# Order of turns of all five engines in a fused cross-attention kernel: one string per engine in place of planned times

## What is computed

```python
# layer 0 (H=16 heads of 16; _fq rounds to 8 bits)
h1 = _ln(x, ln1_g, ln1_b)
x = _attn(h1, h1, a1_wq, a1_wk, a1_wv, a1_wo, a1_bo, ...) + x      # self-attention, 1024 keys
h2 = _ln(x, ln2_g, ln2_b)
x = _attn(h2, context, a2_wq, a2_wk, a2_wv, a2_wo, a2_bo, ...) + x # 77 keys
a, g = jnp.split(_ln(x, ln3_g, ln3_b) @ ff_w1 + ff_b1, 2, axis=-1)
x = a * gelu(g) @ ff_w2 + ff_b2 + x
# layer 1 (16 query heads of 64, 4 key heads, rotary)
q, k = rope(rms(x) @ Wq), rope(rms(ctx) @ Wk)
x = x + softmax(q @ k.T / 8 + mask) @ v @ Wo
y = rms(x)
x = x + silu(y @ Wgate) * (y @ Wup) @ Wdown
```

## Time and profile before

| | us |
|---|---|
| median of 3 runs | 2564.54 (2559.13 to 2568.57) |
| profiled execution | 2568.71 |
| its span, first to last instruction | 2566.9 |
| PE busy in it | 2000.9 (78%) |
| DVE busy | 1802.5 (70%) |
| ACT busy | 1135.9 (44%) |
| POOL busy | 936.3 (36%) |
| mean granted clock of TensorE | 0.874 of full speed |

### The profile page before, as it was taken

How to read it: one execution, slowest core, us unless ns; L and a number is a source line. 1 busy time by engine, 2 the same in 40 slices (tenths; PEclk the granted TensorE clock), 3 DMA queues, 4 the chain that set the end, 5 groups by cost and what they waited for, 6 DMA issues and landing times.

```text
span 2566.9 us, 35318 instructions
## 1 busy us (share of the span) xinstructions
PE 2000.9 (78%) x10552; PEld 1439.1 (56%) x10552; DVE 1802.5 (70%) x3327; ACT 1135.9 (44%) x1906; POOL 936.3 (36%) x1629
## 2 busy tenths in 40 slices
...
GB/s 231 102 162 134 82 121 68 131 62 105 93 81 122 70 134 62 118 76 100 98 71 132 69 135 61 118 78 88 105 77 120 74 120 66 128 55 106 1 36 4
DMA packets 761645, 243.62 MB, mean 95 GB/s; under 512 B 675643, under 2 KB 757295, under 8 KB 761199
## 3 DMA queue, kind: packets, MB, share of 16 engines
q1 hardware_dynamic: 758127, 241.34, 46.3%
...
...
## 4 chain that ended last, share of the span: by engine, by line
PE 47%; DVE 21%; issue 9%; ACT 8%; SPq 5%; DMA 4%; POOL 4%; DVEq 0%; POOLq 0%; ACTq 0%
PE work L1394 21%; PE work L1404 16%; ACT E L899 4%; DVE scaled_row L1055 4%; DVE Pn L1062 3%; PE rowps L1465 3%; DMA PT<-Pn 3%; PE outps L1450 3%; POOL scs L797 2%; SPq L542 1%; DVE st L1078 1%; DVE hids L1202 1%; DVE scs L1144 1%; ACT hTs L875 1%; DVE scs L1216 1%
## 5 line engine op out<-in xcount | busy, mean ns | idle before, releaser
L1055 DVE TENSOR_SCALAR_CACHE_REDUCE scaled_row<-rowps,der 128x1024 uint8<-128x1024 f32 x512 | 654.0, 1277 | 386.8 <-PE rowps L1465 386.5
L899 ACT ACTIVATE E<-rowps,ebias,der 128x1024 f32<-128x1024 f32 x512 | 614.6, 1202 | 392.5 <-DVE scaled_row L1055 312.1
L731 POOL TENSOR_TENSOR rowden<-rowsum,raw 128x1 f32<-128x1 f32 x512 | 113.3, 221 | 943.6 <-ACT E L899 942.3
L1062 DVE TENSOR_SCALAR Pn<-E,rowinv 128x1024 int16<-128x1024 f32 x512 | 389.8, 761 | 89.0 <-DMA PT<-Pn 65.9
L1465 PE MATMUL rowps<-KC,QP 16*128 16x512 bf16 x1024 | 220.8, 428 | 209.5 <-ACT E L899 197.7
L734 POOL TENSOR_TENSOR rowinv<-rowden,minus 128x1 f32<-128x1 f32 x512 | 333.6, 651 | 92.4 <-POOL rowden L731 92.4
L1394 PE MATMUL work<-hTs,ff_w_sb 128*128 128x256 f32 x1024 | 259.9, 409 | 14.2 <-ACT hTs L875 14.2
L1465 PEld LDWEIGHTS rowps<-KC,QP 16*128 16x128 bf16 x1024 | 49.2, 92 | 375.5 <-ACT E L899 244.4
L1394 PEld LDWEIGHTS work<-hTs,ff_w_sb 128*128 128x128 f32 x1024 | 202.3, 204 | 60.0 <-issue 28.4
L1559 PE MATMUL work<-K,hids 128*128 128x154 f32 x1024 | 153.2, 301 | 31.6 <-DVE scs L1216 19.4
L1559 PEld LDWEIGHTS work<-K,hids 128*128 128x128 f32 x1024 | 136.9, 190 | 50.1 <-DVE scs L1216 26.3
...
## 6 DMA issues: line engine op xcount, KB each, us to landing
...
KC<-k_dram SPq DMA_DIRECT2D x128, 64.0 KB, 2.4
...
PT<-Pn SPq DMA_TRANSPOSE x512, 3.1
...
```

Source lines behind the costliest of these rows:

```text
L731: nc.gpsimd.tensor_tensor(rowden[:, n:n + 1], rowsum[:, n:n + 1], raw[:, DW1:DW1 + 1], ALU.mult).then_inc(row_den.sem, 1)
L899: nc.scalar.activation(E[:, slot, :], rowps[n % 2][:], ACT.Exp, bias=ebias[:, n:n + 1], scale=der[:, AL1:AL1 + 1], accum_out=rowsum[:, n:n ...
L1055: nc.vector.tensor_scalar(scaled_row[:, n % 2, :], rowps[n % 2][:], der[:, NAL1:NAL1 + 1], 3.0e38, ALU.mult, ALU.min, accum_out=ebias[:, n ...
L1062: nc.vector.tensor_scalar(Pn[:, n % 2, :], E[:, ring(n)[0], :], rowinv[:, n:n + 1], 255.0, ALU.mult, ALU.min).then_inc(row_round.sem, 1)
```

## The change

The planner goes: `places`, `AT`, `STARTS`, `BEHIND`, `PAIR_GAP` and `Beside` are removed, and an item keeps its name, its evicting engine and the number of its turns on PE. In their place stand five strings. Each letter gives one turn to one part of that engine: p, l, h are pre, low and high; r and v rows and values on PE; b and n maxima and roundings on DVE, s the sums of high's softmax, now a part of its own with its own semaphore; e and o exponentials and outputs on ACT; i inverses on POOL; t the row turns of SP. `take_turns` runs them. Every `yield` with a time becomes a bare `yield`. The banks follow the order of the starts in PE's string. Pre before step 0, and step 0 with its setup, are still merged by times (`by_time`), with pre's times kept in `PRE_AT`. A part that a step lacks is skipped in the string.

```diff
+PRE_ITEMS = [("tr", "A", 1), ("q", "A", 1), ("k", "A", 1), ("v", "A", 2)]
...
-BEHIND = {("high", "down"): ("low", "g", 0.1)}
-STARTS = {"pre": 2.0, "low": 2.0 * LAG + 3.5, "high": 0.5}
-US_PER_HALF = 1.85
-PAIR_GAP = 2.0
...
+TURNS = {
+    "PE": (
+        "vrhhhrrphprprvpphrrhhhhllhrhhrhhhhrhvlrrvlhhhrllhhrhhhhrhllrhrhhhrvrlrlvhrllhhhhvrrlllllhlrllhrhhlrv"
+        "rlllllrrhrrllrl"),
+    "DVE": (
+        "nnpbpnbbnhnbbhnbbhnnhhhlbhhbhhhnhbnlhnhssnbnbhssllbnbhhnblnlbbnnbhbbnnlhllnlbllnblblnnhblnnlhbhhbbnn"
+        "nblbnnhbbnllbl"),
+    "ACT": ("eeepeeppeehpoeeeeehhhllhehheoleheheeeeoehllhleehhhllelleeelleellleoee"),
+    "POOL": ("iipiihpiiliiilhhhiliihhhlhhiiippiiiihiillilliiilhhhlhiiiiiii"),
+    "SP": ("tttthlhlhhtlttpthhthtttptttttttttppttttttttttth"),
+}
...
+PRE_AT = {"tr": (4.0, 4.9), "q": (5.5, 6.9), "k": (6.3, 7.8), "v": (7.2, 8.7)}
...
-AT, ORDER = places(2 * ROWT - 1.5)
+def item_order():
+
+    begins = {c: {sum(x[2] for x in ITEMS[c][:i]): i for i in range(len(ITEMS[c]))} for c in ITEMS}
+    turn, out = {c: 0 for c in ITEMS}, []
+    for letter in TURNS["PE"]:
+        c = PARTS_OF.get(letter)
+        if c:
+            if turn[c] in begins[c]:
+                out.append((c, begins[c][turn[c]]))
+            turn[c] += 1
+    return out
...
+def take_turns(order, parts):
+
+    for part in parts.values():
+        next(part)
+    for letter in order:
+        if letter in parts:
+            next(parts[letter], None)
+    assert all(next(part, "end") == "end" for part in parts.values())
...
+        def run_step(parts, eng, v, order, attention, setup, pre, low, high, sums=None):
...
+            use = dict(attention) if parts["attn"] or parts["old"] else {}
+            for letter, part, d in (("p", pre, LEAD), ("l", low, -1), ("h", high, -2), ("s", sums, -2)):
+                if parts[PARTS_OF[letter]] and part:
+                    use[letter] = part(eng, v + d, runs)
+            take_turns(order, use)
...
             for n in range(4):
-                yield at("sc2", 2 * n + 1) + 1
+                yield
                 l_diff.wait(act, u, n + 1)
...
-            yield from beside_each_other(sums(0), scores(1))
-            yield from beside_each_other(sums(1), products())
+            yield from scores(1)
+            yield from products()
...
+        def high_sums(dve, u, runs):
+
+            for n in range(4):
+                yield
+                h_exp.wait(dve, u, n + 1)
+                nc.vector.tensor_reduce(lsum[:, 1, n, :], sc1[:, n], AX.X, ALU.add).then_inc(h_sums.sem, 1)
+                h_sums.wait(dve, u, n + 1)
+                nc.vector.reciprocal(rsum[:, 1, n, :], lsum[:, 1, n, :]).then_inc(recip_ready.sem, 1)
```

More of the change, by code:

```diff
@@ L60 @@
+    + [("pt1", "A", 1), ("pt1", "D", 1), ("pt1", "A", 1), ("pv1", "D", 4), ("tr3", "A", 1)]
+    + [("gate", "A", 1)] * 4 + [("up", "D", 1)] * 4 + [("down", "D", 1)])
 ITEMS = {"pre": PRE_ITEMS, "low": LOW_ITEMS, "high": HIGH_ITEMS}
-STARTS = {"pre": 2.0, "low": 2.0 * LAG + 3.5, "high": 0.5}
 BANKS = 3
-US_PER_HALF = 1.85
-PAIR_GAP = 2.0
+PARTS_OF = {"p": "pre", "l": "low", "h": "high", "s": "high"}
+TURNS = {
[9 more added lines that the diff above has]
+}
@@ L462, in all_steps @@
             loop(U + 1, U + 2, high=True)
-        def side(parts, eng, v, pre=None, low=None, high=None, setup=None):
+        def run_step(parts, eng, v, order, attention, setup, pre, low, high, sums=None):
             runs = [c for c in ITEMS if parts[c]]
             if parts["setup"]:
-                return Beside(setup(), later(pre(eng, v + LEAD, runs)))
-            return Beside(*[f(eng, v + d, runs) for c, d, f in (("pre", LEAD, pre), ("low", -1, low), ("high", -2, high))
-                            if parts[c] and f])
+                by_time(*attention.values(), setup(), later(pre(eng, v + LEAD, runs)))
+                return
+            use = dict(attention) if parts["attn"] or parts["old"] else {}
[3 more added lines that the diff above has]
+            take_turns(order, use)
         def ring(n):
@@ L688, in step @@
             def step(v, parts):
[L689 to L692 removed]
+                run_step(parts, sp, v, TURNS["SP"], {"t": attn_sync(sp, v, parts)}, setup_sync, pre_sync, low_sync, high_sync)
                 if parts["setup"]:
@@ L847, in step @@
             def step(v, parts):
-                beside = side(parts, pool, v, pre_pool, low_pool, high_pool, setup_pool_part)
-                if parts["attn"] or parts["old"]:
-                    attn_pool(pool, v, parts, beside)
-                beside.rest()
+                run_step(parts, pool, v, TURNS["POOL"], {"i": inverses(pool, v, parts)}, setup_pool_part, pre_pool, low_pool, high_pool)
                 if parts["setup"]:
@@ L1019, in step @@
             def step(v, parts):
-                beside = side(parts, act, v, pre_act, low_act, high_act, setup_act_part)
-                if parts["attn"] or parts["old"]:
-                    attn_act(act, v, parts, beside)
-                beside.rest()
+                run_step(parts, act, v, TURNS["ACT"], {"e": exponentials(act, v, parts), "o": outputs(act, v, parts)},
+                         setup_act_part, pre_act, low_act, high_act)
                 if parts["setup"]:
```

370 lines of the change are left out of this document (147 added, 223 removed), and 3 rows, old and new, of the table HIGH_ITEMS.

## The result

| | before | after |
|---|---|---|
| median, us | 2561.84 (2552.72 to 2568.57, 4 runs) | 2384.26 (2383.5 to 2388.16, 4 runs) |
| profiled execution, its span | 2568.7, 2566.9 | 2384.92, 2383.1 |
| mean granted clock | 0.874 | 0.892 |

The ratio is 0.933, 95% interval 0.930 to 0.936. The direction was right, the size was not, and the named rival "more than forecast" (2375) came nearest.

The account below looks back on a forecast made before the run. Waits between engines bound it, DVE holding PE in one stretch and PE holding DVE in another. Ten full steps at 8.1 us less plus four at 3.8 give 96 us off 2564.5, so 2469 us; range 2410 to 2560.

Parts of the forecast that it names:

- more than forecast: Rival: DVE's blocks overlap everywhere, so the period is 130.5 us and the time 2375; chance 0.08.
- the 3.6 us a step for the low clock: PE at half clock: gate1 +1.9, q2 +1.0, 0.7 for the rest, taking 133.9 to 137.5 us a step.
- (a): PE, Ptr to Pq: ffo.3 and Pq ahead of row 5 cover Ptr's eviction; gain 3.9 us.
- (b): Rows come in pairs on PE, giving DVE two rows where it would idle; no cost where DVE has a backlog.
- (d): Low softmax moves later, up0 ahead of o2, a0 and rows 29 and 30 ahead of down; last evictions lie beside the gates.
- The walk: Pricing of one step of the new order, block by block with step 7's lengths: 133.9 us at full clock.
- (c): ACT: exponentials of rows 10 and 11 stand ahead of hex0 to hex2; hex0 and hex1 wait 6.89 us and longer for POOL.
- E10: ACT's exponential of row 10: ran at 1110.35 behind hex0 and hex1; foretold to stand ahead of them.
- (e): SP sends T0 and T1 before the tables and K2, V2, K1, and k, v stores after T18; costed at nothing.
- (f): POOL casts k and v after I14; costed at nothing, as ACT next uses those buffers a step later.
- (g): high_sums swaps two links for a semaphore of its own; same two instructions, costed at nothing.
- Slower by the clock: Rival: half clock from pt0_0 to gate1 makes a step 149 us and the time 2631; chance 0.12.

Follow-up runs that it names:

- d17: New kernel with three useless DVE operations a step ahead of row 17's maximum, where DVE never idles: 2409.99 us against 2384.26.
- d29: New kernel with three useless DVE operations a step ahead of row 29's maximum, where DVE waits 1.19 us anyway: 2379.44 us against 2384.26.
- t_down: New kernel with only row 30 moved back behind the down product on PE: 2453.8 us, ratio 0.959 to the kernel before.
- h1: New order of all engines up to the first wq, old order for the rest of the step: 2523.25 us, ratio 0.988 to the kernel before.
- x1: h1 with one swap on ACT, the exponential of row 10 ahead of hex0 and hex1: 2523.9 us against 2523.25.
- x5: New order up to q2, old behind it, but ACT's exponentials of rows 10 and 11 back behind hex1 and hex2: 2444.33 us against 2452.16 without that.
- e1: New kernel's machinery with the five strings spelling the old order of every engine: 2562.44 us, ratio 1.002 to the kernel before.
- f_new: New kernel with useless PE products ahead of tr0 and tr3 to keep the clock up: 2380.92 us against 2384.26.
- f_old: Kernel before with useless PE products ahead of rows 5, 19, 20, sc2_7 and q2: 2535.82 us, ratio 0.990.

## Why the prediction was wrong, point by point

The direction and most of the mechanism were right. Two terms of the sum failed: DVE's 122 us of blocks a step, which measured 112.7, and the 3.6 us a step for the low clock, where the runs show next to nothing.

**What bounds the kernel.** Right as far as shown. That DVE sets wq0 to gate0 is shown by d17. From row 23 on DVE has slack for 0.7 us (d29) and not for 5 (t_down); that PE sets the pace there is read from its busy time (38.5 of 43.2 us).

**(a) Ptr and row 5.** Right in size: 5.9 us of that stretch in step 7 against 5.5. Not seen: alone, half of it is given back in the stretches behind it (h1).

**(b), (d) Pairs, softmax, down.** The mechanism is shown for down (t_down). The walk had it: 43.9 with pt2, measured 43.2. The pairs and the low softmax alone were not tried.

**(c) ACT.** Wrong as a reason for a gain. E10 did come earlier by 9 us, and this is worth nothing (x1, x5). The gain of that stretch comes from what PE and, as inferred, DVE do first.

**(e) SP.** Wrong. It was costed at nothing, because the tables still arrive in time. Only the moved tables and stores were looked at, and not T2, which now stands behind five table loads: in step 7 it is issued 3.9 us behind N2, before 2.0. SP by need takes 19.5 us less. This error works against the miss: without it the time would have been still further below the range.

**(f), (g).** Costed at nothing. (g) is covered by e1 (1.002); (f) alone was not tried.

**The walk's size.** These are the two terms that make the miss.

First, DVE's blocks. The walk charged 122 us; the windows have 112.7 busy in step 7. From start to next start, or to its own end if that comes first, the trace has:

| us in step 7 | walk | trace |
|---|---|---|
| 32 maxima with read-out | 43.5 | 38.8 |
| 32 roundings | 24.6 | 26.1 |
| the rest | 53.9 | 47.8 |
| idle | 12 | 17.5 |
| period | 134 | 130.2 |

Two maxima back to back show the slot:

```profile
1063.61 1.25 DVE L1019 TENSOR_SCALAR_CACHE_REDUCE scaled_row<-rowps,der 128x1024 uint8<-128x1024 f32 x1
1064.79 0.08 DVE L1019 DVE_READ_ACCUMULATOR scaled_row<-rowps,der 128x1 f32 x1
1064.79 1.28 DVE L1019 TENSOR_SCALAR_CACHE_REDUCE scaled_row<-rowps,der 128x1024 uint8<-128x1024 f32 x1
1065.99 0.08 DVE L1019 DVE_READ_ACCUMULATOR scaled_row<-rowps,der 128x1 f32 x1
```

They start 1.18 and 1.20 apart, not 1.36: the read-out runs beside the next, and each operation starts before the last one's recorded end. That was there to be read in the earlier trace rows: the walk's check compared 13.7 us of lengths with the 13.5 us of the stretch, but of these DVE was busy only 12.58, and gaps of under 0.25 us (0.94 in all) filled the rest:

```profile
1130.40:1143.92 13.52, 9.01 (x58) 5.94 (x56) 12.58 (x25) 6.06 (x10) 3.08 (x8) 0.93 0.35 69
```

So the lengths were 9% too long (13.7 against 12.58), as over the whole step 8% (122 against 112.7). Of the 9.3 us too many a step, 5.5 came back as more idle time and 3.7 remained. By stretch these 3.7 are 0.8, 0.2, 1.6, 0.3 and 0.7, so only half of them lie where DVE is full. That the lengths are the cause of all 3.7 is argued from this sum, not shown by a run.

Second, the clock. 3.6 us a step were added for gates and q2 at the low level. gate0 and q2 did take 3.75 and 3.42 us (gate1, charged with 1.9 more, ran in 2.18), but the period did not grow: f_new, with gate0 at 1.97 in every step, gets back 3.3 us in the whole execution, not 3.6 a step, and the steps with a slow q2 are the short ones. Nor does the old order show the 5 to 9 us a step that the prediction laid to the clock there: f_old gets 1.7 back, net of its useless products. The cover was in the walk itself: behind q2 it had a wait of 1.5 us for the probabilities, and after q2's 3.42 us 0.48 of it is left. The Trainium skill, "TensorE: Matmul & The Clock Gate", section "HAM oscillation — how this bites in real kernels", says that a kernel pays the half clock again at every gap of a repeating loop. The trace agrees for the blocks in part (gate0 takes 2.66 to 3.75 us in the ten full steps, q2 over 3.4 in four of them), and not for the end time (3.3 us of 2384).

Steps unlike step 7 give 1.5 back: the mean of steps 2 to 11 is 131.7, with 130.2 to 133.1 among them. So 3.7 + 3.6 - 1.5 = 5.8 a step, 58 us in ten. The four steps without pre came out at 129.8 against 136.3, 26 us. (By the walk's own terms, 133.3 + 3.6, it should have been 136.9; the slip is worth 2.4 us in four steps.) The rest, (7.1 - 3.9) for the ends and 3.6 for how the profiled runs stand to the medians, cancels: 84 of the 85 us.

**The rivals.** "More than forecast" came nearest, with a chance of 0.08: its period, 130.5, is within 1.2 of the measured one. Its mechanism, overlap on DVE, is half of the miss; that the clock costs next to nothing is the other half. That its time (2375) is only 9 us off is partly luck: it knew nothing of the 19.5 us that SP's order costs. The number that decides was in hand (recorded busy time 111.0 against 122 charged). "Slower by the clock" needed a penalty of 11.7 us a step over the walk; the period is 2.2 us below the walk.

**What would show it.** Seen as foretold: Pq at 1.9, no wait before row 5, 3.8 us before tr3, 17.3 to 20.1 us idle on DVE in full steps (under 25; before it was 31.2 to 37.7, the prediction's 31 being the least), full steps alike (130.2 to 133.1, before 142.3 to 148.2), E10 no longer behind hex1. Not seen: steps near 137.5. Near to a sign of being wrong that was named, waits of SP for landings: here it is DVE that waits longer for them, by way of SP's order.
